# Softmax over graph edges on one core: each row scanned once each way, outside maxima by a masked maximum, differences before the turn back, exponentials by parts

## What is computed

```python
a = jnp.sum(a * alpha_dot, axis=-1, keepdims=True)
amax = jax.ops.segment_max(a, dst, num_segments=n)
amax = jnp.where(jnp.isfinite(amax), amax, 0.0)
ex = jnp.exp(a - amax[dst])
den = jax.ops.segment_sum(ex, dst, num_segments=n)
alpha = ex / (den[dst] + 1e-16)
...
agg = jax.ops.segment_sum(alpha * h, dst, num_segments=n)
```

## Time and profile before

| | |
|---|---|
| runs | 11963.46, 11967.89, 11981.13 us, median 11967.89 |
| span of the profiled execution, first to last instruction | 7512.8 us |
| its own time | not on the page; the median is 4455.1 us above the span |
| busy in the span | PE 89%, DVE 91%, ACT 68%, POOL 68% |
| mean granted TensorE clock | 0.962 of full speed |
| softmax, from SP's load to the next block's first issue | 4347.38 to 4471.10 us |
| HBM traffic | 967.5 MB, 129 GB/s over the span |

### The profile page before, as it was taken

One profiled execution on the slowest core, in us unless ns is written; L12 is line 12 of the kernel. 1 busy time (PEld: TensorE's weight loads), 2 busy tenths in 40 slices (PEclk: granted clock), 3 DMA queues, 4 the chain that ended last, 5 costly groups with the idle time before them and its releaser, 6 DMA issues. The chain is left out here.

```text
span 7512.8 us, 193248 instructions
## 1 busy us (share of the span) xinstructions
PE 6722.4 (89%) x44602; PEld 5295.6 (70%) x44603; DVE 6803.0 (91%) x15442; ACT 5146.0 (68%) x16654; POOL 5146.0 (68%) x5264
## 2 busy tenths in 40 slices
PE   7588899999989899898999839999899999999997
PEld 4388888888888888888888839996455555555556
DVE  8599999999999999999999978877699999999997
ACT  3277777777777777777777711116688888888884
POOL 3377777777777777777777729860477777777760
PEclk6699999999999999999999969998899999999998
DMA  6454444444444444444444418765455555555556
GB/s 203 126 110 108 108 110 108 110 108 110 108 108 110 108 110 108 110 108 108 109 108 110 104 63 254 224 181 96 114 141 142 142 142 143 142 141 142 142 134 197
DMA packets 971093, 967.50 MB, mean 129 GB/s; under 512 B 452030, under 2 KB 788030, under 8 KB 970942
## 3 DMA queue, kind: packets, MB, share of 16 engines
q0 software_dynamic: 225792, 385.65, 22.6%
q1 hardware_dynamic: 511312, 346.34, 17.1%
q10 hardware_dynamic: 233936, 234.90, 9.4%
HBM read 677.51 MB, written 288.65 MB: 129 GB/s over the span
## 5 line engine op out<-in xcount | busy, mean ns | idle before, releaser
L718 POOL DMA_INDIRECT e_g_src<-table_src,e_idx x1568 | 1542.0, 983 | 505.0 <-issue 477.8
L718 POOL DMA_INDIRECT e_g_dst<-table_dst,e_idx x1568 | 1499.8, 957 | 478.0 <-issue 417.6
L1929 POOL DMA_INDIRECT f_e<-table,f_src x1568 | 1494.5, 953 | 465.7 <-issue 441.4
L755 PE MATMUL e_ps_t<-ident,e_m 128*128 128x128 f32 (+1 forms) x7840 | 1149.9, 277 | 405.3 <-DVE e_m L975 401.2
L1988 PE MATMUL f_ps_a<-sums 128*128 128x384 f32 x3936 | 1402.0, 499 | 1.5 <-DVE sums L2088 1.5
L755 PEld LDWEIGHTS e_ps_t<-ident,e_m 128*128 128x128 f32 (+1 forms) x7840 | 865.1, 139 | 528.9 <-issue 468.7
L1988 PEld LDWEIGHTS f_ps_a<-sums 128*128 128x128 f32 x3936 | 707.7, 190 | 504.7 <-issue 90.3
L848 ACT ACTIVATE e_m1t<-e_ps_t 128x512 f32<-128x512 f32 (+1 forms) x1176 | 692.7, 595 | 337.1 <-PE e_ps_t L755 214.8
L781 PE MATMUL e_ps_v<-e_w_v,e_m1t 128*128 128x64 f32 x3136 | 649.4, 289 | 0.0
L812 PE MATMUL e_ps_h<-e_w_h,e_m2t 96*128 96x96 f32 x3136 | 648.8, 289 | 0.0
L811 PEld LDWEIGHTS e_ps_h<-e_w_h,e_m2t 128*128 128x128 f32 x3136 | 507.0, 191 | 189.9 <-issue 189.2
(11 more groups left out here) (270 smaller groups left out, 16566.3 us busy)
## 6 DMA issues: line engine op xcount, KB each, us to landing
edge_values<-e_h ACTq DMA_DIRECT2D x392, 330.0 KB
r_h<-edge_values SPq DMA_DIRECT2D x196, 660.0 KB, 4.1
sums<-sums ACTq DMA_DIRECT2D x492, 192.0 KB
e_g_src<-table_src,e_idx POOLq DMA_INDIRECT x1568
e_g_dst<-table_dst,e_idx POOLq DMA_INDIRECT x1568
f_e<-table,f_src POOLq DMA_INDIRECT x1568
f_rbf<-basis SPq DMA_DIRECT2D x492, 48.0 KB
basis<-t_part SPq DMA_DIRECT2D x42, 448.0 KB, 3.1
```

Source lines behind the costliest of these rows:

```text
L718: pool.indirect_dma_start(out=into[:, r, t, :], out_offset=None, in_=table, in_offset=bass.IndirectOffsetOnAxis(ap=idx[:, r, c:c + 1], axi ...
L755: last = nc.tensor.transpose(ps_t[bank][0:channels, t * P:(t + 1) * P], rows(t), ident[:])
L1929: pool.indirect_dma_start(out=rows_of_units[:, (place * RING + r) * T + t, :], out_offset=None, in_=table, in_offset=bass.IndirectOffsetOn ...
```

## The change

- The target windows are loaded by SP at the end of its part of `edges`, into a tile that is allocated ahead of the `edges` tiles and lives until `reduce_values` ends. POOL's clearing of `sums` waits for DVE's third instruction.
- Four buffers instead of two for the turns in.
- Every row is scanned once for each side and head, forwards from `rows` to `best`, backwards within `best`. The reduction to `broken` is gone. In its place a mask tells for each edge whether its target differs from the one outside the row (`mark_outer`, which overwrites `breaks[side]`): at the row's last position it says whether the row is broken. The maximum from outside, `start`, is entered with `with_outer`: `best = max(mask + start, best)`. The turns of the row ends and their small scan (`carry`) and `take_start` are placed between scans and maxima.
- `centre`: `rows = rows - best` in the turned layout, a head at a time, since `rows` still holds the logits.
- PE turns the differences back, and ACT takes the exponential of each bank and writes it to its part of `logits`. DVE's subtractions and the exponential of the whole are gone.

```diff
@@ edges
             rounds(sp, load)
+            sp.dma_start(dst_i[:], dst_windows).then_inc(windows_in, 16)
@@ softmax
-        dst_i = sb("dst_i", [parts, edges_on + 2], I32)
-        broken = sb("broken", [parts, 2])
+        IN = 4
         @block.gpsimd
+            pool.wait_ge(own, 3)
             nc.gpsimd.memset(sums[:], 0.0).then_inc(cleared, 1)
         @block.tensor
-                if n >= 2:
-                    pe.wait_ge(taken, n - 1)
+                if n >= IN:
+                    pe.wait_ge(taken, n - IN + 1)
...
-            pe.wait_ge(own, SETUP + 2 * PASS)
             for n in range(HEADS * C4):
+                pe.wait_ge(own, CENTRED[hd])
                 if n >= 2:
-                    pe.wait_ge(own, SETUP + 2 * PASS + n - 1)
+                    pe.wait_ge(expd, n - 1)
         @block.scalar
-            act.wait_ge(own, SETUP + 2 * PASS + HEADS * C4)
-            nc.scalar.activation(logits[:], logits[:], ACT.Exp).then_inc(expd, 1)
+            for n in range(HEADS * C4):
+                hd, c4 = n // C4, n % C4
+                act.wait_ge(back, n + 1)
+                nc.scalar.activation(by_tile[:, c4 * 4:c4 * 4 + 4, :, hd],
+                                     ps_out[n % 2][:].rearrange("p (c q) -> p c q", c=4)[:, :, 0:parts],
+                                     ACT.Exp).then_inc(expd, 1)
         @block.vector
-                d.up(nc.vector.tensor_reduce(broken[:, side:side + 1], breaks[side][:], AX, ALU.min))
...
+            def scan(side, hd):
+                if side == 0:
+                    out, step, fed = best[:, hd, :], breaks[0][:], rows[:, hd, :]
+                else:
+                    out, step, fed = best[:, hd, ::-1], breaks[1][:, ::-1], best[:, hd, ::-1]
+                d.up(nc.vector.tensor_tensor_scan(out=out, data0=step, data1=fed, initial=-FAR,
+                                                  op0=ALU.add, op1=ALU.max))
+            def mark_outer(side):
+                outer = 0 if side == 0 else edges_on + 1
+                inner = edges_on - 1 if side == 0 else 0
+                dve.wait_ge(own, d.n)
+                k = d.up(nc.vector.tensor_scalar(breaks[side][:], dst[:, 1:edges_on + 1], dst[:, outer:outer + 1], -FAR,
+                                                 ALU.not_equal, ALU.mult))
+                d.up(nc.vector.tensor_copy(ends[:, side, :], best[:, :, inner]))
...
+            def with_outer(side, hd):
+                dve.wait_ge(own, d.n)
+                d.up(nc.vector.scalar_tensor_tensor(best[:, hd, :], breaks[side][:], start[:, side, hd:hd + 1],
+                                                    best[:, hd, :], ALU.add, ALU.max))
+            def centre(hd):
+                dve.wait_ge(own, d.n)
+                d.up(nc.vector.tensor_tensor(rows[:, hd, :], rows[:, hd, :], best[:, hd, :], ALU.subtract))
...
-            for n in range(HEADS * C4):
-                dve.wait_ge(back, n + 1)
-                part = by_tile[:, c4 * 4:c4 * 4 + 4, :, hd]
-                d.up(nc.vector.tensor_tensor(
-                    part, part, ps_out[n % 2][:].rearrange("p (c q) -> p c q", c=4)[:, :, 0:parts], ALU.subtract))
```

More of the change, by code:

```diff
@@ L1189, in _ @@
                 hd, c4 = n // C4, n % C4
-                if n >= 2:
-                    pe.wait_ge(taken, n - 1)
+                if n >= IN:
+                    pe.wait_ge(taken, n - IN + 1)
                 for j in range(4):
-                    last = nc.tensor.transpose(ps_in[n % 2][0:parts, j * P:(j + 1) * P],
+                    last = nc.tensor.transpose(ps_in[n % IN][0:parts, j * P:(j + 1) * P],
                                                by_tile[:, c4 * 4 + j, :, hd], ident[:])
                 last.then_inc(turned, 1)
-            for side in range(2):
-                pe.wait_ge(own, SETUP + side * PASS + HEADS + 2)
+            for side, marked, done in ((0, BEFORE_MARKED, BEFORE_CARRIED), (1, AFTER_MARKED, AFTER_CARRIED)):
+                pe.wait_ge(own, marked)
                 nc.tensor.transpose(ps_c[0:HEADS, 0:parts], ends[:, side, :], ident[0:parts, 0:parts])
@@ L1230, in _ @@
             d = Count(own, 0, 0)
-            dve.wait_ge(loaded, 16)
-            dve.wait_ge(own, d.up(nc.vector.tensor_copy(dst[:], dst_i[:])))
-            for side in range(2):
-                k = d.up(nc.vector.tensor_tensor(breaks[side][:], dst[:, 1:edges_on + 1],
-                                                 dst[:, 2 * side:2 * side + edges_on], ALU.not_equal))
-                dve.wait_ge(own, k)
-                k = d.up(nc.vector.tensor_scalar(breaks[side][:], breaks[side][:], -FAR, None, ALU.mult))
-                dve.wait_ge(own, k)
-                d.up(nc.vector.tensor_reduce(broken[:, side:side + 1], breaks[side][:], AX, ALU.min))
@@ L1241, in _, with then @@
-            assert d.n == SETUP
-            dve.wait_ge(taken, HEADS * C4)
-            for side in range(2):
-                def scans(initial):
-                    for hd in range(HEADS):
-                        first = -FAR if initial is None else initial[:, hd:hd + 1]
-                        if side == 0:
-                            out, step, fed = best[:, hd, :], breaks[0][:], rows[:, hd, :]
-                        else:
-                            out, step, fed = rows[:, hd, ::-1], breaks[1][:, ::-1], best[:, hd, ::-1]
-                        d.up(nc.vector.tensor_tensor_scan(out=out, data0=step, data1=fed, initial=first,
-                                                          op0=ALU.add, op1=ALU.max))
-                    dve.wait_ge(own, d.n)
-                scans(None)
-                d.up(nc.vector.tensor_copy(ends[:, side, :],
-                                           best[:, :, edges_on - 1] if side == 0 else rows[:, :, 0]))
+            def then(instruction):
+                dve.wait_ge(own, d.up(instruction))
@@ new lines, in mark_breaks @@
+            def mark_breaks(side):
+                then(nc.vector.tensor_tensor(breaks[side][:], dst[:, 1:edges_on + 1],
+                                             dst[:, 2 * side:2 * side + edges_on], ALU.not_equal))
+                then(nc.vector.tensor_scalar(breaks[side][:], breaks[side][:], -FAR, None, ALU.mult))
+            def scan(side, hd):
[5 more added lines that the diff above has]
+                                                  op0=ALU.add, op1=ALU.max))
@@ L1258, in _, with carry @@
                 d.up(nc.vector.tensor_copy(breaks4[:, side, :],
-                                           broken[:, side:side + 1].broadcast_to([parts, HEADS])))
+                                           breaks[side][:, inner:inner + 1].broadcast_to([parts, HEADS])))
+            def carry(side):
                 dve.wait_ge(ended, 2 * side + 1)
```

72 lines of the change are left out of this document (52 added, 20 removed).

## The result

| | before | after |
|---|---|---|
| runs, side by side | 20, from 11888.9 to 12007.8 us | 20, from 11860.1 to 11968.3 us |
| median | 11948.1 us | 11891.4 us |
| ratio after / before | | 0.9960, 95% interval 0.9944 to 0.9976 |
| profiled execution: time, span, clock | not shown, 7512.8 us, 0.962 | 11952.9 us, 11950.9 us, 0.754 |

By the ratio the change is faster by 48 us (0.0040 x 11948.1; 29 to 67 by the interval); the two medians alone lie 56.7 us apart. The predicted 42.5 us lie in the interval, and the sign had its 0.87. The predicted time, 11925.4, and the range of 11912 to 11943 missed 11891.4.

What follows compares the result with a forecast made beforehand. The softmax, between two barriers, was taken as a DVE chain of 123.7 us wholly on the path. Nine terms summed to -42.5 us, taking 11967.9 to 11925.4 us; range 11912 to 11943.

Steps and rivals of the forecast that it cites:

- the sign: Whole kernel: faster 0.87, same 0.10, slower 0.03, with 0.2% (24 us) as about what a measurement can tell.
- Terms 1 to 3: Softmax: load and memset moved, -14.2 us; two reductions dropped, -4.4 us; second scans dropped, -35.3 us.
- Term 4: Softmax: masks of the outside rewritten twice, 1.4 us each with the wait, +2.8 us (2.5 to 4.7).
- Terms 5 and 6: Softmax: eight masked maxima on DVE, +18.6 us; four differences on DVE, +9.3 us.
- Term 7: Softmax, turns of the row ends: PE's trips hidden, DVE pays about 1.2 us a side, -1.9 us.
- Term 8: Softmax's end: turns back and exponential by parts, mostly under DVE, 4.3 us in place of 22.3, -17.9 us.
- Term 9: Edge stage: the load moved there may hold up gathers, 0 to +3.3 us, +0.5 taken.
- scans and memset: Softmax rival: the two exclude each other, DVE ends 14.4 us later, time 11939.8 us; chance 0.12.
- the load collides: Edge stage rival: the load holds up every gather in flight, +5.6 us, time 11931; chance 0.06.
- Slower gathers: Edge stage rival: moved tiles make each POOL indirect issue 22 ns longer, +69 us, time 11994; chance 0.03.
- The edit doesn't reach the time: Rival: 4455 us outside the span move by 20 us or swallow the gain, 11944 to 11992; chance 0.05.

Runs made afterwards that it cites:

- `first_part`: The kernel before with only the load moved and the memset waiting for DVE's sixth instruction; softmax stage 110.0 us.
- `pool_reads`: The kernel after with a POOL copy of 8192 columns of the cleared tile added behind the memset; softmax stage 87.4 us.
- `b_twin`: The kernel before, unchanged, run once more; 11959.4 us, with 11912.0 for the run of before beside it on the same chip.

## Why the prediction was right and wrong

**Right: the difference.** The eight terms that lie in the stage (the ninth is the edge stage's) gave 80.7 us, and it takes 80.8. That it is so close is partly luck, since small misses cancel: the tail is 0.5 us longer than summed, and the two masks cost 0.4 us less.

- Terms 1 to 3 (load and memset, reductions, second scans): 14.2 us before the first compare, as said; `first_part` measured 13.7 for its part, with 0.4 of a wait that only this kernel has.
- Term 4: 1.29 us a mask, 1.35 taken, and the next step starts 1.20 us behind the mask's start, where 1.4 was taken. Terms 5 and 6: 2.35 and 2.29 us for the steps, 2.29 and 2.29 taken.
- Term 7: DVE's copies and small scan take 0.9 us on the first side (0.66 of it between the first two backward scans) and about 1.3 on the second, and nothing waits. The sum said 1.2 for each.
- Term 8: its mechanism was right, and its size a little off. The exponential of a bank is 0.27 us longer than taken, and the tail 4.8 us instead of 4.3. Twelve of the sixteen lie under DVE.
- Term 9: nothing, where 0.5 was taken.
- The rivals: scans and memset don't exclude each other, which `pool_reads` narrows to operations of POOL that write only; the load collides with nothing. Slower gathers did not come: their mean is 951 ns in after for `e_g_src` and 983 before. "The edit doesn't reach the time" fell with the time around the span: there was none. That part of the gain may be lost in the second layer's edge stage, as chip 8 suggests, was no rival of the prediction, and on the chip of the timed runs the interval of 29 to 67 us cannot show it.

**Wrong: the absolute time.** The step that failed is the level that the sum was set on and the width given to it: 11967.9 us with "6 us each way for a median of three such runs". Twenty runs of before spread over 119 us, and their median, 11948.1, lies 19.8 us below that of the three shown, which had happened to fall within 18 us. From 11948.1 the same sum gives 11905.6, which is already below the range's lower end of 11912. The measured 11891.4 is 14 us below that again, inside what the interval of the ratio allows. With half the spread of the twenty runs each way, the range would have been 11866 to 11985.

A second reading was wrong as well, though it moved neither the difference nor the range: "the median of the runs is 11967.9, so 4455.1 us lie around the span. I leave those unchanged". Every profiled execution here that has a time of its own ends 2 us after its span. The gap was between executions at two levels: 7512.8 us at a clock of 0.962 and 11968 us, where the timed runs of after have 0.753 to 0.765. A reader of the profile alone had two warnings: a span and a time that don't belong together, and three runs as the only sign of the spread.

The edge stages are where the runs differ. On chip 6 the first lasted 6765 to 6795 us in four kernels in which it is alike but for one load, on chip 4 6809 to 6863; `middle` ranged from 258 to 328 us over all.

## What to carry over

Set a profile's span against its own time before using a gap between it and the timed runs; if the profile's own time is missing and the mean clock is near 1, suspect that it comes from another level, and forecast the difference rather than the level. Take the spread of a median from no fewer runs than show it: three that agree tell little. This stage between two barriers could be summed from step durations to within a microsecond; POOL's writes can lie under DVE's two-input steps, as the memset does here under the scans, but the same memset holds up a cast, and a POOL copy, which reads, holds up a mask. Check a gain in one stage against the length of the others too: it can be given back there.

## What the hardware showed beyond that

- **Late starts at an alternating clock.** At the level of the timed runs the edge stages lose more than PE's longer busy time explains: the group of ACT that reads PE's product waits 2065 us on a releaser that the trace can't name, and before's profile has no such wait. Waits of ACT in after, and in before:

```profile
ACT e_ps_v L868 <- remote: 2065.3, 280, 35.4
```

```profile
ACT e_ps_v L867 <- PE e_ps_v L782: 565.4, 381, 2.0
```

One such place in the timeline of after, the last product recorded for that step and its reader:

```profile
4003.48 0.39 PE L783 MATMUL e_ps_v<-e_w_v,e_m1t 128*128 128x64 f32 x2
...
4010.82 0.26 ACT L868 ACTIVATE e_ps_v<-e_ps_v 128x128 f32<-128x128 f32 x1 [8.39 <-remote]
```

The matmuls' ends are modelled, so the 6.95 us between may be work that the model puts too early, or a pause of PE. What holds PE back there is open. `b_twin` has it too (2059.4 us), so it isn't the change's.
- **Half clock under load.** Above: 57 to 207 us of it from the start of `middle`, for the same code and with PE at work in most of it.
- **A wait that was hidden comes out when its cover goes**, as small as 0.42 us, in `first_part`.
